# Fillers of TensorE in the gated layers moved out of the counting rounds and behind them

## The reference

```python
def gated(x, cfc_w, bn_w, bn_b):               # three times, x = x + gated(gn(x), ...)
    xf = x.reshape(b, c, h * w)
    u = jnp.stack([mean(xf), max(xf), std(xf, ddof=1)], axis=-1)
    med = jnp.median(u.reshape(b, -1), axis=-1)[:, None, None]
    u = (u - med) ** 3
    z = jnp.einsum('bck,ck->bc', u, cfc_w)
    z = z / jnp.sqrt(1.0 + 1e-5) * bn_w + bn_b
    return x * jax.nn.sigmoid(z)[:, :, None, None]

def scan_layer(feature, conv_w, conv_b, prelu_a):   # last: x = x + scan_layer(gn(x), ...)
    Wc = conv_w[:, :, 0, 4]                         # 1024 x 1024
    def step(prev, x_i):                            # over columns, forward and then back
        y = jnp.einsum('oc,nch->noh', Wc, prev) + conv_b[None, :, None]
        y = jnp.where(y >= 0, y, prelu_a * y)
        return y + x_i, y + x_i
    ...
```

## Time and profile before

| | |
|---|---|
| median of 3 runs | 872.35 us (872.04 to 872.4) |
| the profiled execution | 872.76 us, span 871.0 us |
| mean granted clock of TensorE | 0.986 of full speed |
| TensorE busy | 834.7 us, 96% of the span |
| VectorE busy | 660.3 us, 76% |
| ScalarE busy | 412.4 us, 47% |
| fillers L572 | 104 in the first 190 us, 435 ns each on average |
| warm-ups L660 | 16, 500 ns each on average |

### The profile page before, as it was taken

How to read it: one execution, slowest core, us unless ns; L and a number is a source line. 1 busy time by engine, 2 the same in 40 slices (tenths; PEclk the granted TensorE clock), 3 DMA queues, 4 the chain that set the end, 5 groups by cost and what they waited for, 6 DMA issues and landing times.

```text
span 871.0 us, 13669 instructions
## 1 busy us (share of the span) xinstructions
PE 834.7 (96%) x4003; PEld 660.5 (76%) x4003; DVE 660.3 (76%) x1433; ACT 412.4 (47%) x1375; POOL 68.4 (8%) x109
## 2 busy tenths in 40 slices
PE   6767699999999999999999999999999999999998
PEld 6632278888888888888888888888888888888886
DVE  6977777866767667677677777888777878778787
ACT  5864314455444454444544445444454444544444
POOL 8864300000000000000000000000000000000000
PEclk9998889999999999999999999999999999999999
DMA  8950200000000000000000033322333223332233
GB/s 347 421 201 1 97 24 1 0 0 0 0 0 0 0 0 0 0 0 0 0 0 0 0 97 96 91 62 88 96 96 96 63 82 96 96 96 70 75 97 97
DMA packets 70510, 56.34 MB, mean 65 GB/s; under 512 B 1888, under 2 KB 66400, under 8 KB 68448
## 3 DMA queue, kind: packets, MB, share of 16 engines
q1 hardware_dynamic: 70064, 56.10, 19.4%
q10 hardware_dynamic: 432, 0.07, 0.0%
HBM read 39.39 MB, written 16.78 MB: 64 GB/s over the span
## 4 chain that ended last, share of the span: by engine, by line
PE 88%; DVE 4%; DMA 3%; SPq 2%; ACT 1%; POOL 1%; issue 1%; POOLq 0%; DVEq 0%
PE ps_prods L667 27%; PE ps_prods L673 26%; PE ps_prods L670 26%; PE ps_turns L689 6%; DMA x_sb<-x_cols 3%; SPq L295 2%; ACT stage L493 1%; PE ps_below L660 1%; DVE below_flags L933 1%; DVE cells L944 0%; PE ps_values L621 0%; POOL pairs L395 0%; PE ps_group L632 0%; PE ps_second L649 0%; PE ps_second L639 0%
## 5 line engine op out<-in xcount | busy, mean ns | idle before, releaser
L667 PE MATMUL ps_prods<-w_hi,s_hi 128*128 128x512 f32 (+1 forms) x1000 | 403.7, 404 | 0.0
L670 PE MATMUL ps_prods<-w_lo,s_hi 128*128 128x512 f32 (+1 forms) x1000 | 402.8, 403 | 0.0
L673 PE MATMUL ps_prods<-w_hi,s_lo 128*128 128x512 f32 (+1 forms) x1000 | 393.0, 393 | 0.0
L520 ACT ACTIVATE act_buf<-ps_prods 128x256 f32<-128x256 f32 x247 | 81.5, 382 | 356.2 <-PE ps_prods L673 356.2
L1038 DVE SCALAR_TENSOR_TENSOR x_sb<-act_buf,x_sb 128x256 f32 (+1 forms) x247 | 105.2, 426 | 154.7 <-ACT act_buf L527 144.9
L673 PEld LDWEIGHTS ps_prods<-w_hi,s_lo 128*128 128x128 f32 x1000 | 188.5, 189 | 38.7
L667 PEld LDWEIGHTS ps_prods<-w_hi,s_hi 128*128 128x128 f32 x1000 | 188.0, 188 | 38.4
L670 PEld LDWEIGHTS ps_prods<-w_lo,s_hi 128*128 128x128 f32 x1000 | 188.7, 189 | 33.2
L527 ACT ACTIVATE act_buf<-ps_turns,bias 128x128 f32<-128x128 f32 x494 | 156.4, 376 | 51.7 <-PE ps_turns L689 51.7
L533 ACT ACTIVATE ps_below<-ps_turns,neg_bias 128x128 f32<-128x128 f32 x494 | 151.8, 361 | 0.0
L1045 DVE SCALAR_TENSOR_TENSOR x_sb<-ps_below,neg_slope,x_sb 128x256 f32 (+1 forms) x247 | 118.9, 481 | 5.2
(11 more groups left out here) (177 smaller groups left out, 347.1 us busy)
## 6 DMA issues: line engine op xcount, KB each, us to landing
x_sb<-x_cols SPq DMA_DIRECT2D x16, 1024.0 KB, 21.8
stage<-x_cols SPq DMA_DIRECT2D x31, 512.0 KB, 4.1
out_cols<-x_sb SPq DMA_DIRECT2D x31, 512.0 KB, 4.8
w_raw<-w_t SPq DMA_DIRECT2D x8, 512.0 KB, 21.2
x_sb<-x_cols SPq DMA_DIRECT2D x1, 2048.0 KB, 8.0
out_cols<-x_sb SPq DMA_DIRECT2D x4, 128.0 KB, 2.2
params<-gates ACTq DMA_DIRECT2D x1, 60.0 KB, 5.3
bias<-conv_bias ACTq DMA_DIRECT2D x1, 4.0 KB, 7.5
```

The lines of the kernel that those rows point to most:

```text
L520: act.activation(act_buf[:, half], ps_prod[c if bank is None else bank][:, half], ACT.Copy) .then_inc(raw_copied, 1)
L667: pe.matmul(out, s_hi[:, k, :], w_hi[:, k, w_cols], start=(k == 0), stop=False)
L670: pe.matmul(out, s_hi[:, k, :], w_lo[:, k, w_cols], start=False, stop=False)
L673: return pe.matmul(out, s_lo[:, k, :], w_hi[:, k, w_cols], start=False, stop=(k == CT - 1))
```

## The change

Only counts of fillers change. In layers 1 and 2, 15 instead of 14 stand behind the group sum L607. In all three layers: 0 instead of 2 in each of the seven counting rounds, 8 instead of 2 behind the last count, 2 instead of 1 behind the turn, 10 instead of 5 behind the median. Of the 104 filler matmuls 104 - 42 + 18 + 3 + 15 + 2 = 100 are left.

```diff
                 if layer > 0:
-                    keep_warm(6, ps_warm)
+                    keep_warm(7, ps_warm)
                 keep_warm(8, ps_warm)
...
                 for k in range(ROUNDS - 1):
-                    keep_warm(2, ps_warm)
                     pe.wait_ge(act_counted, layer * ROUNDS + k + 1)
...
                     .then_inc(floors_ready, 1)
-                keep_warm(2, ps_warm)
+                keep_warm(8, ps_warm)
                 pe.wait_ge(tops_ready, layer + 1)
...
                     .then_inc(tops_turned, 1)
-                keep_warm(1, ps_warm)
+                keep_warm(2, ps_warm)
                 pe.wait_ge(median_ready, layer + 1)
...
                     .then_inc(median_spread, 1)
-                keep_warm(5, ps_warm)
+                keep_warm(10, ps_warm)
```

## The result

| | before | changed |
|---|---|---|
| median | 871.84 us (870.42 to 873.06, 9 runs) | 874.53 us (874.11 to 875.37, 9 runs) |
| profiled execution | 872.76 us, span 871.0 | 875.37 us, span 873.6 |
| mean granted clock | 0.986 | 0.980 |

The ratio is 1.0033, with a 95% interval of 1.0023 to 1.0042: the changed kernel is 2.0 to 3.7 us slower. The forecast was 875.8, or +3.4 over the 872.35 known then.

What follows compares the result with a forecast made beforehand. TensorE, mostly the untouched scan, bounds the kernel; counting rounds are a latency chain set by ScalarE's count. Terms 0.75 + 3.5 - 0.3 - 0.26 - 0.28 = +3.4 us gave 875.8 us, with an 8-in-10 range of 873.1 to 877.9.

Steps and rivals of the forecast that it cites:

- The direction and the mechanism: Emptied rounds lose the clock sooner, the eight fillers run mostly slow and delay the turn: slower by over 0.2%, 83%.
- The burst: Behind the last count: seven of eight fillers run at 1.2 GHz and delay the turn, +3.5 us, between 0 and +4.1.
- The rounds: Counting rounds: without fillers, 15 run at 1.2 GHz, each 0.05 us longer; +0.75 us, between 0 and +1.7.
- Turn and median: Behind the turn, two fillers for one: clock up in two layers, late in one; -0.3 us, between -1.6 and +1.3.
- The ten and the fifteen: Fillers behind the median and behind the group sum: both stay hidden, the ten with the clock up; 0 us each.
- a sign of being wrong: Before the group sum: the forecast is wrong if group sums start right behind the tenth filler; no size given.
- The end: Ahead of the scan: third group sum at 2.4 GHz, -0.26 us; warm-ups end sooner until VectorE limits, -0.28 us.
- The sum up to the scan: All terms from counting rounds to the scan's start: 0.75 + 3.5 - 0.3 - 0.26 - 0.28 = +3.4 us.
- The rival of a clock that survives: Counting rounds: their matmuls hold the clock up and the eight fillers fit; -1.4 to -2.1 us; chance 5%.

Runs made afterwards that it cites:

- both kernels with other warm-ups: Kernel before with 8 instead of 16 warm-ups: 873.33 us, ratio 1.0001; changed kernel with 24 instead of 16: 876.94 us, ratio 1.0041.
- full rounds: Against the kernel before: 4 fillers per counting round, 8 behind last count, 2 behind turn, 10 behind median, 14 behind group sum: 868.65 us, ratio 0.9957.
- four instead of eight: Changed kernel with 4 instead of 8 fillers behind the last count: 874.82 us, ratio 1.0014 against the kernel before.
- only filled rounds: Kernel before with 4 instead of 2 fillers in each counting round, nothing else changed: 872.64 us, ratio 0.9994.
- full rounds with a full first norm: The kernel with full rounds, plus 7 instead of 2 fillers behind the first group sum (L602): 868.55 us, ratio 0.9962 against the kernel before.

## Why the prediction was right, and where its sizes were off

**The direction and the mechanism** were right. The rounds had work on TensorE that cost nothing and kept the clock up longer. With it gone, the clock falls sooner. It had been down at the last count before the change too, and so the eight fillers meet it in either case: they run at 1.2 GHz, outlast the 2.03 us that VectorE gives them, and hold the turn. Eight alone give 1.0029, the empty rounds alone 1.0002, and eight with a full clock 0.9957: the cost is the burst's, and the clock decides it. The emptied rounds add little to it, 4.42 us for the bursts against 3.85 with the rounds' fillers kept.

**The burst** was put at +3.5 us with one of eight fillers at 2.4 GHz. It measured +4.42 and, in the second trace, +4.28, a little above the upper end of 4.1. This is the term that was mis-sized. The clock came back later than I took it: in four of the six bursts the turn came 3.60 us behind the last count, all eight at 1.2 GHz. The upper end itself was short, since eight at 1.2 GHz took 3.53 us from the first filler to the turn (66.38 to 69.91), and not 3.40.

**The rounds** were put at +0.75 and cost +0.33. The count of rounds at the low clock was nearly right, 14 against the 15 taken. A round grows by 0.02 us and not by 0.05: at 1.2 GHz the matmul of 34 columns took 0.21 instead of 0.19. It had no row before, and the scaling from the 72-column matmul overshot.

**Turn and median** were put at -0.3. They came to +0.53 and -0.41, +0.12 together, since the pair of fillers met 1.2 GHz in two layers and not in one. **The ten and the fifteen** cost nothing, as forecast: with 0.31 us of waiting left before the group sum twice and none the third time. There the group sum started right behind the tenth filler, which the prediction had named as a sign of being wrong; it cost nothing, since the piece from median to group sum was 3.07 us against 3.06 before, and the second trace of the changed kernel had 0.22 us of waiting left. **The end** was put at -0.54 and gave -0.62; the 16 warm-ups stopped setting the scan's start, and VectorE's waits took back most of what L666 gained. The kernel with 8 warm-ups shows the same limit by itself: 1.09 us at the first matmul, 0.38 left at the first turn. But only the 0.26 of the group sum is safely the change's, since the copy of before had the rest (13.15 us instead of 13.53) without an edit.

**The sum up to the scan** was +3.4 and measured +4.24 in the trace, and +3.76 by the first turn of the second trace (130.15). That the time came out at +2.6 to +2.9, and so near the forecast, is in part luck, owed to something not in it: the scan was 1.62 us shorter in the trace after. Since one and the same program gave 738.95 and 740.26 us, this is not safely the change's. Whether the change shifts how often the shorter scan comes is open. Of thirteen traces seven had 740.2 to 740.7 us: before, its copy, the empty rounds, eight alone, both kernels with other warm-ups, and full rounds the second time. Six had 738.9 to 739.1: the changed kernel twice, full rounds, four instead of eight, only filled rounds, and full rounds with a full first norm. Entering the scan behind VectorE does not set it, since the kernel with 8 warm-ups did so and had 740.66.

**The rival of a clock that survives** described, with its 1.4 to 2.1 us of gain, what full rounds then did: 2.46 us up to the scan, 3.0 in the median. In the changed kernel itself it fell away: with the rounds empty, TensorE never idled for more than 1.00 us in them, and the clock was down from 57.4 us on.

## What to carry to other kernels

A filler is free only while it fits a wait, and whether it fits depends on the clock: price each burst at the low level, here 0.44 us a filler (eight in 3.53 us), and compare it with the wait it lies in. Fill the waits that cost nothing first, here the counting rounds, where two more fit; a burst behind thinly filled rounds started at half speed here, and its fillers took 0.44 us each instead of 0.22. A change of fillers has to be judged along the whole chain, since full rounds alone and a long burst alone brought nothing or a loss, and both together 0.4%.

## What the runs showed of the hardware

The clock did not fall or rise at the same place in two executions of one program: it fell at 65.1 and at 66.7 us in the first layer of before. Where the place moves, the time moves with it: before took 870.2 to 873.2 us over 29 runs, the kernel with eight fillers alone 870.7 to 876.3, and in both the slower runs tend to have the lower mean granted clock. Full rounds, whose clock stays up, took 868.53 to 868.84, and the second time 868.38 to 869.06 but for one run of 870.0, whose trace has the long scan. A clock that changes need not scatter: the nine runs of the changed kernel lie within 874.11 to 875.37. And the clock is not all of it. The median of before was 871.68 us beside the first four experiments and 873.15 beside the next four, on one chip and at nearly the same granted clock (median 0.982 and 0.984); what made this difference is open.

The scan's back-to-back matmuls have more than one rhythm at the same granted clock of 1.00. A step of 48 matmuls took 12.03 us in some stretches and 12.07 in others, and in the long scans partly a mix of both. From 130 to 850 us their starts were 232.96 ns apart on average before and 232.27 after (the mean over the gaps between 220 and 250 ns). It can switch within an execution. Over 61 steps the long scans and the short ones lie 1.1 to 1.8 us apart. What sets it was not found.
